# Order of score pairs: the causal maximum taken in two halves, sliding maxima first, first queries fetched with the keys

## The reference, cut to what matters

```python
# layer 0
h = rmsnorm(layernorm(x)) * norm_w
lin   = linear attention, causal, Taylor features of (h Wq Wqf, h Wk Wkf): scores (0.5 s + 1)^2-like, row sums divide
slide = softmax over keys t-64..t of (h Wq)(h Wk)^T / sqrt(D)
x = x' + [lin, slide] @ Wout + ffn(...)        # three ternary layers, silu gate, two gelus
# layer 1
causal = softmax over keys 0..t of q k^T / sqrt(D), q, k, v from layernorm(x)
y = x + causal @ Wo
y += sum over the top 2 of 8 experts: gate_e * (gelu(xn @ W1[e] + b1[e]) @ W2[e] + b2[e])
```

## Time and profile before

| | |
|---|---|
| runs, median (lowest to highest) | 1449.33 us (1446.84 to 1457.99), 3 runs |
| the profiled execution | 1449.49 us, span 1447.7 us, mean granted TensorE clock 0.954 |
| busy, share of the span | PE 1281.5 us (89%), PEld 883.7 (61%), DVE 817.4 (56%), ACT 705.5 (49%), POOL 604.2 (42%) |
| opening, first sequence | to 64.7, to 185.6 us |
| six sequences of the loop | start at 185.6, 331.9, 478.0, 625.1, 770.6, 915.4 us |
| last sequence, tail, expert tiles | from about 1060, 1187 and 1283 us to the end |

### The profile page before, as it was taken

The page is one execution under the profiler, slowest core; times in us unless marked ns, Lnnn a source line. Parts: engine busy times, 40 slices in busy tenths (PEclk is TensorE's granted clock), DMA queues, the critical chain, the costliest instruction groups (busy, mean ns, idle before and its releaser), DMA issues. The chain is left out here.

```text
span 1447.7 us, 28890 instructions
## 1 busy us (share of the span) xinstructions
PE 1281.5 (89%) x9082; PEld 883.7 (61%) x9082; DVE 817.4 (56%) x3372; ACT 705.5 (49%) x1511; POOL 604.2 (42%) x793
## 2 busy tenths in 40 slices
PE   4987989998999899989998999899989945679997
PEld 2555556655665666566656665566556733469997
DVE  4055367636763676367636763676367546446663
ACT  2355246724662466246624662467245600447765
POOL 6023143415342444244424342434243536238787
PEclk9998999999999999999999999999999965699998
DMA  9302330234022402240224022402240035024443
GB/s 262 92 2 74 79 106 8 82 71 113 10 82 57 127 10 80 53 133 10 75 59 133 10 74 59 133 10 74 59 129 11 10 88 165 3 37 67 60 66 46
DMA packets 82246, 102.07 MB, mean 71 GB/s; under 512 B 12472, under 2 KB 43104, under 8 KB 82016
## 3 DMA queue, kind: packets, MB, share of 16 engines
q1 hardware_dynamic: 60160, 80.24, 20.4%
q0 software_dynamic: 14304, 10.61, 4.7%
q10 hardware_dynamic: 7632, 9.31, 2.1%
HBM read 55.44 MB, written 46.37 MB: 70 GB/s over the span
## 5 line engine op out<-in xcount | busy, mean ns | idle before, releaser
L940 ACT ACTIVATE probs<-bank 128x512 f32<-128x512 f32 (+2 forms) x896 | 440.3, 579 | 350.2 <-PE bank L566 345.5
L566 PE MATMUL bank<-K,Q 128*128 128x192 f32 (+4 forms) x1024 | 236.7, 323 | 44.5 <-issue 16.3
L1111 POOL TENSOR_SCALAR_AFFINE_SELECT probs<-probs 128x384 f32<-128x384 f32 x256 | 127.1, 519 | 330.7 <-ACT probs L940 299.7
L566 PEld LDWEIGHTS bank<-K,Q 128*128 128x128 f32 x1024 | 171.5, 196 | 89.2 <-DVE mx_c L1313 33.1
L566 PE MATMUL bank<-Q,K 128*128 128x192 f32 (+4 forms) x1024 | 212.4, 324 | 12.9 <-DMA Q<-mrow_c 8.5
L623 PE MATMUL heads<-probs,V 128*9 128x192 f32 (+4 forms) x3072 | 197.4, 398 | 17.7 <-DVE probs L1362 5.9
L566 PEld LDWEIGHTS bank<-Q,K 128*128 128x128 f32 x1024 | 152.2, 197 | 42.2 <-issue 23.7
L930 ACT ACTIVATE probs<-bank,sh_s 128x512 f32<-128x512 f32 x64 | 44.0, 687 | 228.3 <-PE bank L559 207.2
L623 PEld LDWEIGHTS heads<-probs,V 128*9 128x9 f32 x3072 | 76.8, 91 | 128.1 <-issue 83.8
L1173 POOL DMA_INDIRECT out<-h1T_s x78 | 123.5, 1583 | 47.3 <-issue 26.9
L566 PE MATMUL bank<-QM,K 128*128 128x512 f32 (+3 forms) x512 | 131.6, 347 | 12.2 <-DVE mx_c L1313 3.9
(11 more groups left out here) (190 smaller groups left out, 2052.2 us busy)
## 6 DMA issues: line engine op xcount, KB each, us to landing
Q<-slots_of_q SPq DMA_DIRECT2D x16, 1024.0 KB, 8.6
K<-slots_of_k SPq DMA_DIRECT2D x64, 192.0 KB
QM<-slots_of_qm SPq DMA_DIRECT2D x8, 1024.0 KB, 9.1
slots_of_q<-Q SPq DMA_DIRECT2D x24, 256.0 KB, 3.0
slots_of_k<-QM SPq DMA_DIRECT2D x24, 256.0 KB, 4.1
slots_of_qm<-Q SPq DMA_DIRECT2D x24, 256.0 KB, 4.3
slots_of_k<-Q SPq DMA_DIRECT2D x24, 256.0 KB, 3.0
slots_of_q<-Q ACTq DMA_DIRECT2D x24, 256.0 KB, 4.8
```

Source lines behind the costliest of these rows:

```text
L566: mm = pe.matmul(to[:, at:at + right.shape[1]], left, right, start=True, stop=True, skip_group_check=True)
L940: return act.activation(to, bank, func, scale=scale, bias=bias).then_inc(taken_sem(run, unit), 1)
L1111: pool.affine_select(out=three, in_=three, compare_op=ALU.is_ge, fill=0.0, base=0, pattern=[[0, 3], [1, P]], channel_multiplier=-1)
```

## The change

`linear_stage` and `causal_stage` become one `pairs_stage`. Two counts run through it: d over the maxima, a over the scores (0 to 39 linear, 40 to 79 causal). With causal work the maxima are 12 sliding, 40 causal, 20 sliding; in the first sequence they are the 32 sliding ones. `scores_by` says how many scores are issued before maximum d. The third layer comes at d = 8 (d = 0 in the first sequence), the prefix after d = 5. The causal maximum of heads 0 to 7 is turned and placed after d = 34, that of heads 8 to 15 after d = 54, into the two halves of Q2; causal units 0 to 19 wait for the first, 20 to 39 for the second. VectorE takes `weigh_experts` ahead of all maxima and `place_rows` after the sixth. ScalarE instead of VectorE copies causal heads 0 to 2. The q1 fetch moves behind qm1's, the parts of q2 and k2 move from Q1 to Q2, and the GELU of `h2_2` goes between ScalarE's second and third send of q2. In the tail causal scores start beside maximum 30, `list_tiles` comes at causal unit 12, and pads are sent two behind each causal mask.

```diff
-LEAD, BEHIND = 12, 8
-def linear_by(n):
-    return LEAD + (n + 1) * (PAIRS - LEAD - BEHIND) // PAIRS
-def smax_by(n):
-    return BEHIND + min(len(SMAX_UNITS) - BEHIND, 5 * (n + 1) // 6)
+HALF = PAIRS // 2
+AHEAD, LEAD = 12, 8
+def maxima(before):
+    sliding = [("smax", n) for n in range(len(SMAX_UNITS))]
+    return sliding[:AHEAD] + [("cmax", n) for n in range(PAIRS)] + sliding[AHEAD:] if before else sliding
+def scores_by(before, d):
+    if not before:
+        return 8 + (PAIRS - 8) * d // (len(SMAX_UNITS) - 1)
+    return LEAD * d // AHEAD if d < AHEAD else LEAD + 61 * (d + 1 - AHEAD) // 60
+def third_at(before):
+    return 8 if before else 0
+def turned_by(d):
+    return {AHEAD + HALF + 2: 0, AHEAD + PAIRS + 2: 1}.get(d)
...
+def tail_scores_by(n):
+    return max(0, n - HALF - 9)
...
-        mx_c, mx_s = sb("mx_c", [P, P]), sb("mx_s", [P, P])
+        mx_c, mx_s = sb("mx_c", [P, 2, H * NT // 2]), sb("mx_s", [P, P])
...
-                    "q2": (Q1[:, 0, :], Q1[:, 1, :]), "k2": (Q1[:, 2, :], Q1[:, 3, :])}
+                    "q2": (Q2[:, 0, :], Q2[:, 1, :]), "k2": (Q2[:, 2, :], Q2[:, 3, :])}
...
+            def place_causal(run):
+                for n in range(2):
+                    place_max(run, f"causal_max{n}", mrow_c[n], Q2[:, G // 2 * n:G // 2 * (n + 1), :], "placed_c")
...
                     fetch_sent((b, 1), "qm1")
+                    fetch_sent((b, 1), "q1")
...
                     fetch_sent((b, 0), "k2")
-                    if after:
-                        sp.wait_ge(S["sent_q1"], due("sent_q1", (b, 1), SENT))
                     fetch_sent((b, 0), "q2")
-                if after:
-                    if this:
-                        sp.wait_ge(S["slots_q2"], due("slots_q2", (b, 0), 16))
-                    fetch_sent((b, 1), "q1")
...
+            def causal(run, sequence, n):
+                if n % HALF == 0:
+                    pe.wait_ge(S["placed_c"], due("placed_c", sequence, PLACED * (n // HALF + 1)))
+                tri_scores(run, CAUSAL_UNITS, K2b, Q2, n)
...
+                for d, (kind, n) in enumerate(maxima(before)):
+                    while a < scores_by(before, d):
+                        linear(a) if a < PAIRS else beside_causal(a - PAIRS)
+                        a += 1
+                    if d == third_at(before):
+                        third_layer(run)
+                    if (kind, n) == ("smax", 0):
+                        pe.wait_ge(S["slots_q1"], due("slots_q1", now, 16))
+                    if (kind, n) == ("cmax", 0):
+                        pe.wait_ge(S["slots_k2"], due("slots_k2", previous, PLACED))
+                        pe.wait_ge(S["slots_q2"], due("slots_q2", previous, 16))
+                    slide_max(run, n) if kind == "smax" else causal_max(run, n)
+                    if d == 5 and before:
+                        prefix(run, previous)
+                    if (kind, n) == ("cmax", 7):
+                        turn_gates(run, previous)
+                    if before and turned_by(d) is not None:
+                        turn_causal_max(run, turned_by(d))
+                while a < 2 * PAIRS:
+                    beside_causal(a - PAIRS)
+                    a += 1
...
+                    if n in (18, 28, 38) and before:
+                        copy_heads(previous, CAUSAL, n // 10 - 1)
...
                     for s in (0, 1):
                         act.dma_start(view[s], high.bitcast(F32)).then_inc(S["sent_q2"], 16)
+                    if after:
+                        gelu(run, "h2_2", hidden_c[2], sh2[:, 2:3])
                     act.wait_ge(taken_sem(run, "q2"), taken_at(run, "q2"))
...
-            send_pads()
+            pool.wait_ge(S["pads_counted"], 1)
             for p in range(H // 2):
                 mask_tri(("tail", NB), (LAST, 0), CAUSAL, CAUSAL_UNITS, p)
+                for n in range(K2):
+                    send_pad(K2 * p + n)
...
             def tail_stage(run):
                 previous = (LAST, 0)
+                weigh_experts(previous)
                 place_rows(run, previous)
...
                 for n in range(PAIRS):
+                    while a < tail_scores_by(n):
+                        beside_scores(a)
+                        a += 1
                     causal_max(run, n)
-                    if n == 1:
-                        weigh_experts(previous)
                     if n == 7:
                         take_gates(run)
-                negate_max(run, "causal_max", mrow_c)
-                list_tiles()
-                for g in range(G):
-                    copy_heads(previous, CAUSAL, g)
-                    divide_rows(run, previous, CAUSAL, g)
+                    if n == HALF + 2:
+                        negate_max(run, "causal_max0", mrow_c[0])
+                for a in range(a, PAIRS):
+                    if a == 12:
+                        negate_max(run, "causal_max1", mrow_c[1])
+                        list_tiles()
+                    beside_scores(a)
```

360 lines of the change are left out of this document (168 added, 192 removed).

## The result

| | kernel before | kernel after |
|---|---|---|
| runs, median (lowest to highest) | 1448.47 us (1446.84 to 1457.99) | 1409.39 us (1406.67 to 1411.87) |
| the profiled execution | 1449.49 us, span 1447.7 | 1411.42 us, span 1409.7 |
| ratio after to before | | 0.971, 95% interval [0.968, 0.974] |

The change gains 39 us where 66 were forecast: the right side and inside the range, 26 us short of the number. I count in periods that both kernels have: from one copy of a new V by VectorE (`V<-bank,bv`) to the next, and in the tail from the last of them to the first bias matmul of the output (`b_s,gatesT_s`). The last column is the same account in series 3 of the experiments, where both kernels ran again.

The account below looks back on a forecast made before the run. VectorE was taken to pace the pair stage's middle and TensorE its end, 9.5 us a sequence lost. Gains of 35 (sequences) + 4 (GELU) + 7 (first sequence) + 20 (tail) = 66 us, 1449.5 to 1383 us; 80% range 1360 to 1420.

Parts of the forecast that it names:

- (a): Pair stage, seven sequences: new order of maxima and scores gains 5.0 us a sequence (bounds 1.5 and 7.5), 35 in all.
- the first rival: Causal stretch of the pair stage: VectorE still paces the middle, 1.5 us a sequence, 1408 us; chance 0.18.
- PE can run seven banks ahead, to 333.7, so this costs little: Start of the pair stage: TensorE fills seven banks to 333.7 while VectorE weighs experts until 333.4; little cost.
- (c): GELU of h2_2 ahead of the last q2 send: TensorE's 0.68 us wait goes seven times, 4 us (bounds 0 and 8).
- (b): First queries fetched with the keys: the 1.30 us wait for q2 queries goes, cover 1.8 us; no separate gain.
- (d): Causal head copies on ScalarE and halved maxima: covered, with 2 to 3 us left for the halves; gain nothing.
- (e): First sequence: sliding maxima spread over the linear part instead of trailing it, 7 us (bounds 4 and 9).
- (f): Tail: pads two by two behind masks, causal scores beside maximum 30; gain 20 us (bounds 5 and 28).
- the hole: Tail's causal maxima: 16.7 us of slow VectorE instructions, idle on issue, where POOL sends sixteen pads back to back; forecast to go.
- Pads crawl along: Rival for the tail: pads make VectorE crawl in the causal part too, tail gain 5, 1398 us; chance 0.10.
- VectorE crawls in every sequence: Slower rival: row sends beside k2 and q2 fetches make VectorE crawl each sequence, 117 us more, 1500 us; chance 0.05.
- More headroom: Rival for pair stage and tail: TensorE headroom judged by weight loads, 6.9 us a sequence, 28 in tail, 1362; chance 0.06.

Follow-up runs that it names:

- series 3: Third sitting, on one chip: kernel before unchanged again 1435.09 us, kernel after unchanged again 1408.33 us, ratio 0.983.
- weigh late: Kernel after with VectorE's weigh_experts behind the fourth sliding maximum instead of ahead of all maxima: 1400.19 us, ratio to before 0.975.
- linear units first: Kernel after with its first eight linear units ahead of the first sliding maximum: 1388.92 us, ratio to before 0.968.
- series 1: First sitting, on one chip, of kernel before and kernel after: 1448.47 and 1409.39 us, ratio 0.971.
- pads later: Kernel before with only the tail's sixteen pads sent two behind each causal mask instead of ahead of the masks: 1442.68 us, ratio 1.005.
- the variants: Edited versions of the kernel after, among them third layer at d = 0 with the list of tiles in two halves: 1378.11 us, ratio to before 0.960.

## Why the prediction was right, and where it was wrong

**(a) Order of pairs: mechanism right, size half.** The causal stretch is TensorE's and not VectorE's (35.03 of 35.3 us), so the first rival, whose 1408 us is the time that came out, is not the reason for it. The step that failed is "PE can run seven banks ahead, to 333.7, so this costs little", with VectorE "free at 333.4". VectorE's first maximum was to come 1.5 us behind TensorE's start. It comes 3.1 to 4.0 us behind it in the five stages that the loop's jump leads to, and 5.8 and 5.9 us in the two others. In the two others that is POOL's power, and 2.3 to 2.4 us of small instructions for the 1.4 of the estimate. In the loop VectorE is also gone by itself, for 4.2 to 5.4 us where nothing of POOL's is ahead of it (weigh late); in the kernel after it takes up the routing 0.9 to 2.3 us behind the end of POOL's power there, and 0.15 us behind it outside the loop. The trace of before has no row for it, since VectorE waited for TensorE's prefix there; but it has TensorE's own pause at the same place, 2.06 us idle on "issue", and I gave VectorE none. That the late VectorE was covered by twelve linear units, which the change thins out, is the cover that the text should have named. Seven banks are no reserve either: TensorE has filled them 2.2 us after its start in the last sequence and 3 us after it in the second of the loop. The wait itself is small, 15.2 us in seven; the clock makes it larger: 0.61 over 13.1 us. In the 20 us from 4 us after each new V the clock is halved for 61.2 us in all seven, 17.1 in the kernel before. Half of the difference, 22 us, is an estimate of what that costs, if TensorE sets the pace there; the seven sequences are 19 us short of (a) and (c). With linear units first the sequence gains 5.8 us against the kernel before in its series (145.9 to 140.1), and 5.6 were forecast for (a) and (c).

**(b)** right: no wait for `slots_of_q` is left. **(c)** the wait went as said (12.5 to 5.7 us after, to 3.7 alone), and alone brings 2.6 us or nothing instead of 4. The step that failed is that a wait which goes is time which goes: TensorE's pause at the loop's restart, 3.4 us in five before, is 10.6 in the kernel with this part alone and 11.4 in the kernel after. **(d)** right: in the loop nobody waits for a half that is turned late. **(e)** 5.0 and 6.5 us for 7, inside its bounds; the turn of the sliding maxima was forecast near 102, its matmul comes at 104.18 instead of 109.51.

**(f) Tail: 15.5 us for 20, but most of it for one reason only.** The crawl goes when the pads do: right in series 1, where the forecast was made. What failed is the rest of the sum, the 3.3 us and more that should come from the overlap, and the assumption that the hole is a property of the kernel. All but the crawl together brought 1.1 us. The first mask comes 25.3 us after the first maximum, as forecast within a microsecond, but the chain from the first mask to the end of the eighth takes 32.1 us for the 28.7 of 1.4 + 7 x 3.9, and the slow clock in the last weighing 2.1 for the 1 to 2 allowed. With the list of tiles split the chain takes 29.3 us and the tail is 4.5 shorter. I had put the list under "no idle on issue" and never asked what queues behind its 9.4 us. The pads between the masks were in the sum; the trace of pads later puts their price at some 6 us. In a sitting without the crawl the same forecast of 66 us would have met 26: that the whole came out inside the range is in good part luck.

By the sentence that the forecast took from the Trainium skill, fetches are hidden and the hole has another cause. Its conclusion that the tail might then gain only the overlap was wrong in series 1 and right in series 3. Of the cause itself no row decides: between 1197 and 1232 us the two queues that carry instructions move two packets and one, in the crawling trace of before and in the other one alike. The Trainium skill ("SBUF — State Buffer", Who interferes with whom) also lets VectorE and GpSimd lock each other out at a shared port, but not where VectorE's instruction has at most one input in SBUF and is outside the two-port modes. A maximum has one such input; no row tells its mode; and the same instructions in the same order crawl in series 1 and not in series 3, so that rule alone does not give it either.

**Rivals.** "Pads crawl along" and "VectorE crawls in every sequence" did not come. "More headroom" (6.9 us a sequence, 1362) did not come either: the variants ended at 5.8 to 6.0 us a sequence and 1378, close to the forecast itself.

**Open:** what the condition for the crawl is; whether pads two by two are always safe under it; whether the fetches at the loop's start cause the pause; and what share of the thin start's cost is VectorE's own absence, as no run takes it away. Nothing here tries them.

## What to carry to other kernels

Before work is put at the start of a loop body, look how long each engine is away there, in the idle time on "issue", and what each waits for before its first instruction; a wait that is taken away just ahead of the restart may come back as pause. Give TensorE a few microseconds of dense work that needs none of the late ones; in these traces a thin start cost it the clock for longer than the gap, in the loop and outside. Beside every piece that moves onto an in-order engine, name what stands behind it, as the list of tiles stood before the heads. And when a large part of a forecast rests on one odd stretch of one trace, take a second trace of the same kernel in another sitting before believing it.

## What the hardware showed that was not expected

- Where the loop begins anew TensorE pauses 1.6 to 3.2 us in the kernel after and VectorE 4.2 to 5.4 in the one with `weigh_experts` late, waiting for nothing shown; straight-line code between the same two stages has 0.86 for VectorE, and there it waits for a bank.
- TensorE's pause in five restarts was 3.4 us in sum behind 6.5 us of waits for ScalarE, and 10.6 with those waits gone.
- Beside sixteen row scatters that POOL issues in 20 us VectorE may take 45 us for forty maxima instead of 28, with the same instructions and in the same order.
- The kernel before took 1452.51 and 1433.11 us in two sittings on one chip. In the slower one its variants were traced with the crawl; that the faster had none is taken from the time alone.
- After the pause at the loop's start the granted clock of the next 13.1 us is 0.87 where dense work follows and 0.61 where the same engine's work is thin; without a pause, in the last sequence, thin work brings 6.8 us at 1.2 GHz.
